# Eight ranked keys per list, Gelu a batch later, and values weighed at once, in attention and product-key experts

## What is computed

```python
x = x + attention(layernorm(x))     # 16 heads of 8 features, one shared k and v, causal
x = x + experts(layernorm(x))
# experts, for each token and each of 8 heads:
sx, ix = top_k(sim[0], 16)          # 32 x keys
sy, iy = top_k(sim[1], 16)          # 32 y keys
scores, pk = top_k(sx[:, None] + sy[None, :], 16)       # the best 16 of all pairs
h = gelu(xn . down[indices]) * softmax(scores)
out = sum(h * up[indices])
```

## Time and profile before

| | |
|---|---|
| median of 3 runs | 1045.94 us |
| the profiled execution | 1047.43 us |
| its span | 1045.6 us |
| mean granted TensorE clock | 0.887 of 2.4 GHz |
| busy: TensorE | 766.0 us (73%) |
| busy: VectorE | 862.4 us (82%) |
| busy: ScalarE | 712.7 us (68%) |
| busy: GpSimd | 644.5 us (62%) |

### The profile page before, as it was taken

How to read it: one execution, slowest core, us unless ns; L and a number is a source line. 1 busy time by engine, 2 the same in 40 slices (tenths; PEclk the granted TensorE clock), 3 DMA queues, 4 the chain that set the end, 5 groups by cost and what they waited for, 6 DMA issues and landing times.

```text
span 1045.6 us, 22349 instructions
## 1 busy us (share of the span) xinstructions
PE 766.0 (73%) x6066; PEld 482.5 (46%) x6066; DVE 862.4 (82%) x4054; ACT 712.7 (68%) x1040; POOL 644.5 (62%) x371
## 2 busy tenths in 40 slices
PE   3772868777877878787778878787878778776374
PEld 2431535454554645454455545444545546353243
DVE  2316298998989899899989899989989897988987
ACT  1352686877778686878867786868787786847371
POOL 2111069494958768594939677694949486675851
PEclk9686888899998989898998989898999989897766
DMA  5322103021211103020212112030212111000000
GB/s 148 50 24 35 17 9 43 1 40 15 39 16 35 20 9 47 0 52 3 40 15 39 16 21 34 8 47 0 43 12 39 16 34 18 1 12 2 5 1 10
DMA packets 51538, 26.51 MB, mean 25 GB/s; under 512 B 5168, under 2 KB 51120, under 8 KB 51312
## 3 DMA queue, kind: packets, MB, share of 16 engines
q1 hardware_dynamic: 51504, 26.11, 15.1%
HBM read 19.93 MB, written 5.24 MB: 24 GB/s over the span
## 4 chain that ended last, share of the span: by engine, by line
DVE 38%; PE 34%; issue 16%; ACT 8%; DMA 1%; SPq 1%; POOL 1%; DVEq 1%; ACTq 0%; POOLq 0%
DVE prob L930 13%; PE misc L1156 7%; PE score L1136 5%; PE score L1217 4%; ACT prob L650 4%; DVE late_scores L792 4%; DVE cand_left L894 4%; PE misc L1158 3%; PE score L1138 3%; DVE best L888 3%; DVE best L902 2%; DVE cand L873 2%; PE misc L1245 2%; DVE halves L786 2%; PE score L1229 2%
## 5 line engine op out<-in xcount | busy, mean ns | idle before, releaser
L451 POOL TENSOR_TENSOR acc<-acc,prob 128x1024 f32<-128x1024 f32 x186 | 440.0, 2366 | 16.6 <-DVE prob L930 0.5
L930 DVE SCALAR_TENSOR_TENSOR prob<-score,cut,prob 128x1024 f32<-128x1024 f32 x256 | 317.8, 1277 | 39.3 <-ACT prob L650 38.7
L650 ACT ACTIVATE prob<-score,neg_lse,unit 128x1024 f32<-128x1024 f32 x256 | 296.9, 1198 | 36.2 <-PE score L1217 25.5
L1217 PE MATMUL score<-sel,pieces_t 128*128 128x512 f16 x512 | 176.3, 442 | 73.4 <-DVE prob L930 64.0
L562 ACT ACTIVATE probs<-score 128x512 f32<-128x512 f32 x192 | 107.4, 599 | 65.4 <-PE score L1138 63.8
L438 POOL TENSOR_TENSOR pieces<-sim,pieces 128x512 f16<-128x512 f32 x32 | 36.4, 1159 | 145.1 <-ACT pieces L606 145.1
L1136 PE MATMUL score<-q_stack,k_stack 128*128 128x512 bf16 x192 | 76.3, 401 | 45.7 <-DVE prob L930 23.3
L1217 PEld LDWEIGHTS score<-sel,pieces_t 128*128 128x128 f16 x512 | 42.0, 109 | 145.6 <-DVE prob L930 111.7
L1106 PE MATMUL score<-k_ahead,q_ahead 128*128 128x256 bf16 (+1 forms) x512 | 75.8, 253 | 31.0 <-ACT late_scores L545 13.6
L424 POOL TENSOR_TENSOR scale<-bounded,half_neg 128x2 f32<-128x2 f32 x16 | 11.2, 699 | 130.6 <-DVE bounded L833 130.6
L850 DVE MATCH_REPLACE8 left<-top,sim 128x32 f32<-128x32 f32 x512 | 82.8, 173 | 0.0
(11 more groups left out here) (122 smaller groups left out, 1618.9 us busy)
## 6 DMA issues: line engine op xcount, KB each, us to landing
q_ahead<-q_scratch SPq DMA_DIRECT2D x96, 64.0 KB
q_stack<-q_scratch SPq DMA_DIRECT2D x96, 64.0 KB
q_scratch<-qk_piece SPq DMA_DIRECT2D x16, 192.0 KB, 2.4
xin<-x SPq DMA_DIRECT2D x16, 128.0 KB, 4.4
xres<-x SPq DMA_DIRECT2D x16, 128.0 KB, 4.8
out<-fin SPq DMA_DIRECT2D x16, 128.0 KB, 5.3
k_ahead<-qk_piece SPq DMA_DIRECT2D x96, 4.0 KB
k_stack<-qk_piece SPq DMA_DIRECT2D x96, 4.0 KB
```

The lines of the kernel that those rows point to most:

```text
L451: eng.tensor_tensor(acc[:, j, :], so_far, prob[:, j * FH + h, :], ALU.add).then_inc(acc_added, 1)
L650: eng.activation(prob[:, g, :], score[g % BUFS][:, :], ACT.Exp, bias=neg_lse[:, j, h:h + 1], scale=unit[:, :]).then_inc(prob_made, 1)
L930: eng.scalar_tensor_tensor(prob[:, g, :], score[g % BUFS][:, :], cut[:, j, h:h + 1], prob[:, g, :], ALU.is_ge, ALU.mult).then_inc(prob_mas ...
L1217: ins = eng.matmul(score[g % BUFS][:, cols], pieces_t[:, j, h, :], sel[:, cols], start=True, stop=True)
```

## The change

**Keys.** `select_keys` ranks only 8 of the 32 keys of a list: 16 MAX8 and, for the y lists, 8 MATCH_REPLACE8 a tile. The pairs that may be among the best 16 are then other ones: `near` holds all 32 x keys with the best y key, the two best x keys with y keys 2 to 8, and x keys 3 and 4 with y keys 2 to 5 (54 a head). The 8 best sums come from `near`. `cand` holds `near` with these 8 replaced, x keys 5 to 8 with y keys 2 and 3, and the best x key with the y keys left over (94 a head), and gives sums 9 to 16. For tile 0 the copy into PSUM takes the x keys too and goes to `misc[1]`. `size` is made from three of the ranked values behind the selection.

**Gelu.** Hidden units and Gelu of batch i-1 run in iteration i, behind the exponentials of the second attention pass; the hidden matmuls read a copy of xn_t (`xn_kept`, made by a DMA) and are spread between the score matmuls. The last batch's stay in its own iteration. The two copies of x2 go from ScalarE to DMAs on the SP queue.

**Values.** Both `piece_transposes` move behind the weighing, into `misc[0]`, and `weigh_values` waits for neither; the keep-busy matmuls of the second pass go. The order of VectorE's, ScalarE's and GpSimd's calls is changed.

SP queue and GpSimd:

```diff
             def iteration(i, d, f, a, m, p):      # sync
+                if d and f:
+                    age_x2(i - 1)
+                if f:
+                    copy_x2(i)
                 if a:
                     load_residual(i + 1)
                 if p:
                     load_x(i + 3)
+                if a:
+                    keep_xn(i)
...
+            def copy_x2(b):
+                eng.wait_ge(x2_made, made)
+                if later(b):
+                    eng.wait_ge(x2_moved, moved)      # age_x2 of the batch before has landed
+                eng.dma_start(x2_kept[:, :, :], x2[:, :, :]).then_inc(x2_copied, 16)
+            def keep_xn(b):
+                eng.wait_ge(xn_t_made, made)
+                if later(b):
+                    eng.wait_ge(hidden, used)
+                eng.dma_start(xn_kept[:, :], xn_t[:, :]).then_inc(xn_kept_in, 16)
...
                     make_xn(i + 1)                 # gpsimd
+                if f:
+                    add_head(i, 0, 1)
+                    add_head(i, 0, 2)
+                if a:
                     sim_low_piece(i + 1, 0)
                     sim_low_piece(i + 1, 1)
                 if f:
-                    add_head(i, 0, 1)
-                    add_head(i, 0, 2)
                     add_head(i, 0, 3)
```

ScalarE, the new order, condensed (the rest of `iteration` stays):

```diff
+                if a:
+                    for u in range(MAX_STEPS):
+                        att_exp(i + 1, u)
+                if d and f:
+                    activate(i - 1, 0)
+                    activate(i - 1, 1)
                 if a:
                     invert_sums(i + 1)
                 if m:
                     copy_v(i + 2)
+                    max_scores_back(i + 2, 0)
+                    max_scores_back(i + 2, 1)
                     best_exp(i, 0)
+                    max_scores_back(i + 2, 2..4);  pieces_back(i, 0)
+                    max_scores_back(i + 2, 5..8);  log_sum(i, 0);  pieces_back(i, 1)
+                    max_scores_back(i + 2, 9..11)
                 if a:
                     xn_back(i + 1)
+                if f and not a:
+                    activate(i, 0)
+                    activate(i, 1)
+                best_exp(i, 1)
+                pair_probs(i, 0, 0)
+                log_sum(i, 1)
+                pair_probs(i, 0, 1)
+                sim_back(i + 1, 0)
+                pair_probs(i, 0, 2)
+                sim_back(i + 1, 1)
+                sim_high_piece(i + 1, 0)
+                pair_probs(i, 0, 3)
+                sim_high_piece(i + 1, 1)
                 xhat_back(i + 3)
```

VectorE:

```diff
                     select_keys(i, 0)
-                    gate(i - 1, 0)
                     select_keys(i, 1)
                     ln1(i + 3)
-                    make_y(i + 1)
                     sum_pairs(i, 0)
                     select_pairs(i, 0)
+                    make_y(i + 1)
+                    sum_pairs(i, 1)
                     make_x2(i + 1)
+                    gate(i - 1, 0)
+                    sum_best(i, 0)
+                    select_pairs(i, 1)
                     gate(i - 1, 1)
-                    sum_best(i, 0)
+                    log_sum_exp(i, 0)
                     fold_max(i + 2, 0, 6)
-                    sum_pairs(i, 1)
-                    log_sum_exp(i, 0)
-                    select_pairs(i, 1)
+                    sum_best(i, 1)
                     mask(i, 0, 0)
+                    log_sum_exp(i, 1)
                     mask(i, 0, 1)
...
+                tops = ranked[:, j, :, RANK_X:RANK_Y + RANKED]      # sum_pairs
                 if j == 0:
+                    placed = misc[1][:, 0:FH * 2 * RANKED].rearrange("p (h k) -> p h k", k=2 * RANKED)
+                    eng.tensor_copy(placed, tops).then_inc(top_placed, 1)
                     eng.wait_ge(top_placed, every(top_placed, b))
+                    tops = placed
+                eng.tensor_tensor(near[:, :, 0:KEYS], xs, tops_y[:, :, 0:1].broadcast_to([P, FH, KEYS]), ALU.add)
...
+                eng.tensor_tensor(cand[:, :, col:PAIRS], left[:, j, :, :], first_x.broadcast_to([P, FH, KEYS]), ALU.add)
```

TensorE, condensed:

```diff
                     eng.wait_ge(max_t_made, every(max_t_made, i + 1))
-                    for u in range(6):
+                if a and d:
+                    hidden_units(i - 1, 1, range(0, 4), xn_kept)
+                for u in range(MAX_STEPS):
                         scores_for_probs(i + 1, u)
-                        keep_busy(misc[0], 2)
+                        # u < 4: chunk 4 + u of tile 1; u >= 4: chunk u - 4 of tile 0
+                if a:
+                    weigh_values(i + 1, 0, max_t_made, i + 1)
+                    weigh_values(i + 1, 1, max_t_made, i + 1)
+                if m:
+                    scores_for_max(i + 2, 0)
+                    scores_for_max(i + 2, 1)
+                    project_y(i + 1, y_t_made, i + 1)
+                    piece_transposes(i, 0, y_t_made, every(y_t_made, i + 1))
+                    acc_transposes(i - 1, 0)
+                    scores_for_max(i + 2, 2..6)
+                    piece_transposes(i, 1, piece_t_made, at(piece_t_made, i, 1))
+                    scores_for_max(i + 2, 7..8)
                     acc_transposes(i - 1, 1)
+                    scores_for_max(i + 2, 9..11)
+                if f and not a:
+                    hidden_units(i, 0, range(CH), xn_t)
+                    hidden_units(i, 1, range(CH), xn_t)
+                pair_scores(i, 0, 0);  pair_scores(i, 0, 1)
                     xn_transpose(i + 1, piece_t_made, i)
+                pair_scores(i, 0, 2)
                     key_scores(i + 1, 0);  key_scores(i + 1, 1);  xhat_transpose(i + 3, sim_kept, i + 1)
                     pair_scores(i, 0, 3);  pair_scores(i, 0, 4);  project_qkv(i + 3)
```

More of the change, by code:

```diff
@@ L29 @@
 STACK = len(Q_PIECE) * HD
-PAIR_BLOCKS = ((0, 1, 16), (1, 1, 8), (2, 2, 5), (4, 4, 3), (8, 8, 1))
-PAIRS = sum(na * nb for _, na, nb in PAIR_BLOCKS)
+RANKED = 8
+NEAR_BLOCKS = ((0, 2, 1, 7), (2, 2, 1, 4))
+FAR_BLOCK = (4, 4, 1, 2)
+NEAR = KEYS + sum(na * nb for _, na, _, nb in NEAR_BLOCKS)
+PAIRS = NEAR + FAR_BLOCK[1] * FAR_BLOCK[3] + KEYS
+RANK_X, RANK_Y = 23, 31
 BANK = 512
@@ L337, in place_max_row, with age_x2 @@
                 eng.dma_start(row, max_t[:, :]).then_inc(max_row_in, 16)
+            def age_x2(b):
+                copied = held(eng, every(x2_copied, b))
+                read = held(eng, at(fin_made, b, 0))
+                eng.wait_ge(x2_copied, copied)
+                if later(b):
+                    eng.wait_ge(fin_made, read)
+                eng.dma_start(x2_aged[:, :, :], x2_kept[:, :, :]).then_inc(x2_moved, 16)
+            def copy_x2(b):
+                made = held(eng, every(x2_made, b))
+                moved = held(eng, at(x2_moved, b, 0))
+                eng.wait_ge(x2_made, made)
[3 more added lines that the diff above has]
+            def keep_xn(b):
+                made = held(eng, every(xn_t_made, b))
+                used = held(eng, at(hidden, b, 0))
+                eng.wait_ge(xn_t_made, made)
+                if later(b):
+                    eng.wait_ge(hidden, used)
+                eng.dma_start(xn_kept[:, :], xn_t[:, :]).then_inc(xn_kept_in, 16)
             def store(b):
@@ L702, in iteration @@
                     copy_v(i + 2)
-                    for u in range(9):
-                        max_scores_back(i + 2, u)
+                    max_scores_back(i + 2, 0)
+                    max_scores_back(i + 2, 1)
                 if f:
@@ L707, in iteration @@
                 if m:
-                    for u in range(9, MAX_STEPS):
+                    for u in range(2, 5):
+                        max_scores_back(i + 2, u)
+                if f:
+                    pieces_back(i, 0)
+                if m:
+                    for u in range(5, 9):
                         max_scores_back(i + 2, u)
@@ L720, in iteration @@
                     sim_back(i + 1, 0)
-                    sim_back(i + 1, 1)
-                if f:
-                    best_exp(i, 1)
                 if f:
@@ L842, in select_keys @@
                 eng.wait_ge(sim_kept, value)
-                for l in range(LISTS):
-                    eng.max(top[:, j, l, 0:8], keys_of[l]).then_inc(key_step, 1)
-                for half in range(2):
-                    value = held(eng, at(key_step, b, n + (half + 1) * LISTS // 2))
-                    eng.wait_ge(setup_dve, 1)
-                    eng.wait_ge(key_step, value)
-                    for l in range(half * LISTS // 2, (half + 1) * LISTS // 2):
-                        eng.match_replace(left[:, l, :], top[:, j, l, 0:8], keys_of[l], LOWEST).then_inc(key_step, 1)
@@ L851, in select_keys @@
-                n += LISTS
-                for half in range(2):
-                    value = held(eng, at(key_step, b, n + (half + 1) * LISTS // 2))
-                    eng.wait_ge(setup_dve, 1)
-                    eng.wait_ge(key_step, value)
-                    for l in range(half * LISTS // 2, (half + 1) * LISTS // 2):
```

(19 more changed lines are left out.)

203 lines of the change are left out of this document (93 added, 110 removed).

## The result

The changed kernel takes 1056.35 us (median of 4 runs, 1054.54 to 1057.86), beside 1045.01 us for the kernel before on the same chip: 1.0104 times as long, 95% interval 1.0078 to 1.013. It is slower by 1%, where I had forecast 1041 us and a gain.

What follows compares the result with a forecast made beforehand. No engine bounds the kernel everywhere: VectorE carries 38% of the chain, TensorE 34%. Loop +6, iteration 0 -5.5, iterations 13 and 14 -9, iteration 15 +3.5: -5 on 1047.4, itself 1.5 above the median, gives 1041 us; range 1008 to 1060.

Steps and rivals of the forecast that it cites:

- the ends: Outside the twelve loop periods: iteration 0 -5.5, iterations 13 and 14 together -9, iteration 15 +3.5 us.
- Rival A: No blocking of any weight by GpSimd: make_y at +12.95 to +13.85, period 55.2 to 56.1, total 1008; chance 0.2.
- rival D: x lands late, past +8.57, behind age_x2: `ln_tmp` takes +11.0, period 58.9, total 1046; chance 0.13.
- That wait goes, and I expect no such loss after.: TensorE's 2.24 us wait before weighing the values goes, and with it the loss from weighing at 1.2 GHz.
- the loop term: Twelve loop periods at 58.5 us each instead of 58.03: +6 us.
- the forecast was 58.5: Loop period: 57.46, plus 0.6 for a later second exponential, plus 0.5 behind it, gives 58.5 us.
- the +0.5: TensorE's fourth-head scores, queued behind xhat transposes that want both sim_back, cost -0.2 to +1.0 us, taken as +0.5.
- The -9 for iterations 13 and 14: Iterations without ln1, where `shifted` asks at +10.9; 13 also lacks the xhat queue: -6.5 and -2.5 us.
- the 14.8 from tile 1's sums to the exponential: VectorE's chain from tile 1's first add, at +16.8, through gates and fold_max to the second exponential, at +31.6.
- instructions with one tensor in SBUF do not stretch: VectorE instructions beside GpSimd's adds: those with one tensor in SBUF keep their length, as MAX8 and six masks did.
- log_sum(1) waiting 2 to 4 us: ScalarE's logarithm for tile 1, queued ahead of the second exponential, waits 2 to 4 us; named as a sign.
- Rival C: GpSimd takes a turn after each blocked VectorE instruction: tile 1's sums at +18.2, period 59.9, total 1058; chance 0.2.

Runs made afterwards that it cites:

- x1: Changed kernel with GpSimd's head additions cut from 1024 to 16 columns: 997.81 us, ratio 0.9543.
- x6: Changed kernel with SP issuing the load of x ahead of the two copies of x2: 1055.54 us, ratio 1.0092.
- x4: Changed kernel with 28 keep-busy matmuls into a free bank ahead of project_y, during TensorE's wait: 1040.50 us, ratio 0.9956.
- x9: Changed kernel with tile 0's first best sum and size, and tile 1's ranked keys, put into PSUM: 1020.82 us, ratio 0.9773.
- x3: Changed kernel with tile 1's exponential ahead of ScalarE's last three score copies and its sum ahead of fold_max: 1022.32 us, ratio 0.9773.
- x8: Changed kernel with tile 0's operands in PSUM, tile 1's exponential and sum early, 28 keep-busy matmuls and x loaded first: 991.43 us, ratio 0.9483.
- x10: Changed kernel with both tiles' operands in PSUM, tile 1's exponential and sum early, x loaded first, no keep-busy matmuls: 980.40 us, ratio 0.9386.

## Why the prediction was wrong

**Right.** The keys (2.78 a tile); `ln_tmp`, `shifted` held to the ends of adds; "`cut` behind it: 0 if VectorE keeps its turn", 472.09 behind 2.20; make_y at +15.98 for +16.3; Gelu and its table loads free in ScalarE's idle time (463.12 to 467.65, the sums at 468.09); the ends, -13.2 for -11. Rival A's period was x1's (its 1008 was 10 over x1's time, nearly all of it in the ends), and rival D fell with x6.

**The step that failed** is the sentence under "The sum": "That wait goes, and I expect no such loss after." The wait of 2.24 us went; one of 3.73 us for make_y came, and it was in my own numbers: row sums ready at +12.0, make_y at +16.3, nothing for TensorE between but two score matmuls. I had costed 1.2 GHz only in the weighing, where the profile of before showed it. Eleven of twelve periods lose 0.9 to 2.2 us by it: 59.86 - 58.56 = 1.30 on the mean, 12 x 1.30 = 15.6, which is the 16 that the loop term missed. x4 gives the loss back, and x9 shows both states in one run.

**Right by luck.** The one period without this loss lasts 58.56, and the forecast was 58.5; its second exponential starts at +31.73 for +31.6. From there to the eighth mask it is 15.7 for 15.8. But the +0.5 in that 15.8 stood for xhat's queue, and x4 shows what it was: with the same queue the stretch takes 15.1 us in three periods where 1.2 GHz among the masks lasts 6.8 us, as before, and 15.7 in the eight where it lasts 10.2. Without that the period is 58.0, 0.5 under the forecast. The -9 for iterations 13 and 14 was right in sum alone: they are 4.7 and 5.8 shorter (57.58 to 52.85, 57.34 to 51.50), where I had 6.5 and 2.5.

**Smaller misses.** In the 14.8 from tile 1's sums to the exponential I had charged no hold for the sums themselves: 0.82 and 0.65, where x1 has 0.40 and 0.21; that is 0.9, and the earlier start (+16.31 for +16.8) gives 0.5 of it back. The prediction says that instructions with one tensor in SBUF do not stretch; `ln_tmp` is one, and it did, before and after. And I did not see that the logarithm's wait, which I named ("log_sum(1) waiting 2 to 4 us"), was itself removable: x3, which takes it out, is 2.7 a period shorter.

**Rival C's number was right, its reason not.** It gave 1058 by alternating turns from a period of 59.9. The period was 59.86, but tile 1's sums began at +16.31, not +18.2. The alternation exists, though: x8 shows it, where GpSimd has two adds left. In the changed kernel the held instruction met the last add, and only a short instruction (0.75) stood behind it.

What stays open: why iteration 4 keeps its clock after the same 3.74 us wait, as two periods of x6 do (58.57 and 58.60, after 3.73 and 3.76), and why 1.2 GHz among the masks lasts 6.8 us in one period and 10.2 in the next. By the Trainium skill (TensorE: Matmul & The Clock Gate, Part 1) the gate follows TensorE's recent activity on a phase of its own, and not the kernel's; the two kinds of period in x9 would fit that, but no run here varied the phase.

## What to carry to other kernels

When a change moves a wait from one place on TensorE to another, cost what runs behind the new wait at half its clock, unless rows of the same length of wait show otherwise; a few matmuls that compute nothing are then worth trying. Where GpSimd works in long instructions, lay its instruction ends out as a grid, and for each VectorE instruction with all operands in SBUF ask which end it will run to: moving it helps only if it crosses one. And a page's chain may put a fifth on a queue whose late transfer costs nothing, because what it feeds is held anyway.

## What the runs showed of the hardware that was not expected

- After equal waits (3.73 and 3.74 us) TensorE was granted 0.50 in one period and 1.00 in another of the same execution; after 2.0 us in x9, down to 0.50 in eight periods and 1.00 throughout in four; after 2.0 to 2.2 us in x10, 1.00 in all of eleven periods.
- The hold takes the smallest instructions too: `ln_tmp`, 128x2 with one tensor operand, took 1.31, 2.12 and 2.32 us at three places, each time up to an add's end, while MAX8 and the batch norm steps beside the same adds keep their length. By the Trainium skill (SBUF — State Buffer, Who interferes with whom) a `tensor_scalar` can enter a mode that takes the shared ports; these rows are of that kind.
- Turns go back and forth: in x8 two VectorE instructions in a row were each held, 1.42 and 2.55 (two instructions), so GpSimd began its next add between them.
